# Splitting the operands of a feed-forward up projection into high and low parts in a layered attention and recurrence kernel

## What is computed

```python
for i in range(DEPTH):                      # 6 layers
    x = attn_layer(shift_tokens(x), Wqkv[i], ...) + x
    x = ffn_layer(shift_tokens(x), ...) + x
# ffn_layer:
xn = (x - mu) / sqrt(var + 1e-5) * g + bln  # 128 channels
hg = xn @ W1 + b1                           # up projection, 128 -> 2 * 341
a, gate = split(hg, 2, -1)
return a * gelu(gate) @ W2 + b2
```

## Time and profile before

| | us |
|---|---|
| median of 3 runs | 1705.56 (1705.02 to 1705.87) |
| the profiled execution: its own time | 1703.4 |
| its span, first to last instruction | 1701.6 |
| TensorE matmuls busy | 1619.4 (95%) |
| VectorE busy | 1366.9 (80%) |
| GpSimd busy | 1321.8 (78%) |
| ScalarE busy | 1308.0 (77%) |
| TensorE: all records of the up projection (L846, L847) | 171.7, in 576 records |
| mean granted TensorE clock | 0.995 |

### The profile page before, as it was taken

One profiled execution on the slowest core, in us unless ns is written; L12 is line 12 of the kernel. 1 busy time (PEld: TensorE's weight loads), 2 busy tenths in 40 slices (PEclk: granted clock), 3 DMA queues, 4 the chain that ended last, 5 costly groups with the idle time before them and its releaser, 6 DMA issues. The chain is left out here.

```text
span 1701.6 us, 49333 instructions
## 1 busy us (share of the span) xinstructions
PE 1619.4 (95%) x19632; PEld 1360.7 (80%) x19632; DVE 1366.9 (80%) x1999; ACT 1308.0 (77%) x2410; POOL 1321.8 (78%) x1269
## 2 busy tenths in 40 slices
PE   4799999999999999999999999999999999999985
PEld 2678887888888888887888887888888877787774
DVE  5888887888887888887888887888888887877843
ACT  3577788778778878878877877887887878877774
POOL 8888888887879788789788788878878777776630
PEclk9999999999999999999999999999999999999998
DMA  6233332433322333232343232334323222322231
GB/s 195 74 101 87 90 91 65 122 86 105 99 70 86 90 111 114 73 94 77 88 123 97 81 103 65 88 104 122 89 74 93 64 76 76 89 63 64 62 88 28
DMA packets 178175, 151.60 MB, mean 89 GB/s; under 512 B 110751, under 2 KB 149277, under 8 KB 177821
## 3 DMA queue, kind: packets, MB, share of 16 engines
q1 hardware_dynamic: 177948, 148.46, 30.8%
HBM read 22.06 MB, written 1.05 MB: 14 GB/s over the span
## 5 line engine op out<-in xcount | busy, mean ns | idle before, releaser
L1429 POOL TENSOR_TENSOR qk<-qk,t 128x1024 f32<-128x1024 f32 x192 | 458.8, 2390 | 108.3 <-DVE qk L1209 107.4
L1206 DVE TENSOR_TENSOR t<-ps_qn,tab 128x512 f32<-128x512 f32 x384 | 265.0, 690 | 148.9 <-ACT sq L984 136.6
L1441 POOL TENSOR_TENSOR qkr<-qk,rinv 128x1024 f32<-128x1024 f32 x192 | 361.7, 1905 | 7.5
L1020 ACT ACTIVATE qbd<-ps_tr 64x512 f32<-64x512 f32 x384 | 226.9, 591 | 72.5 <-PE ps_tr L735 67.2
L709 PE MATMUL ps_qn<-w_hi,xs_hi 128*128 128x512 f32 x576 | 261.0, 453 | 21.6 <-POOL xs_lo L1478 11.0
L971 ACT ACTIVATE pbd<-ps_tr 64x512 f32<-64x512 f32 x384 | 226.1, 589 | 66.5 <-PE ps_tr L722 63.6
L984 ACT ACTIVATE sq<-ps_qn 128x512 f32<-128x512 f32 x384 | 228.5, 595 | 43.8 <-PE ps_qn L711 38.9
L1209 DVE TENSOR_TENSOR qk<-ps_qn,tab 128x512 f32<-128x512 f32 x384 | 261.5, 681 | 0.0
L711 PE MATMUL ps_qn<-w_hi,xs_lo 128*128 128x512 f32 x576 | 228.3, 396 | 0.0
L710 PE MATMUL ps_qn<-w_lo,xs_hi 128*128 128x512 f32 x576 | 228.3, 396 | 0.0
L1219 DVE TENSOR_REDUCE ss<-sq 128x32 f32<-128x2048 f32 x96 | 216.7, 2257 | 0.0
(11 more groups left out here) (147 smaller groups left out, 3010.5 us busy)
## 6 DMA issues: line engine op xcount, KB each, us to landing
v_own<-v_new SPq DMA_DIRECT2D x96, 512.0 KB, 3.2
v_back<-v_new SPq DMA_DIRECT2D x96, 384.0 KB, 3.5
v_back<-v_own SPq DMA_DIRECT2D x96, 128.0 KB, 2.3
kT<-kT SPq DMA_DIRECT2D x84, 128.0 KB, 2.7
w_raw<-in_Wqkv SPq DMA_DIRECT2D x18, 512.0 KB, 5.3
xsh<-x SPq DMA_DIRECT2D x192, 32.0 KB, 2.3
fx<-xmid SPq DMA_DIRECT2D x96, 64.0 KB, 2.1
wo<-in_Wo SPq DMA_DIRECT2D x6, 512.0 KB, 3.8
```

Source lines behind the costliest of these rows:

```text
L1206: v.tensor_tensor(t2[:, part].rearrange("p (h s d) -> p h s d", s=2, d=DH // 2), swapped, tab[:, 2 * k + 1:2 * k + 2, :].rearrange("p o (s ...
L1429: g.tensor_tensor(qk[b][:, part], qk[b][:, part], t2[:, part], ALU.add).then_inc(added[b], 1)
L1441: g.tensor_tensor(qkr[b][:, part].rearrange("p (h d) -> p h d", d=DH), qk[b][:, part].rearrange("p (h d) -> p h d", d=DH), rinv[b][:, k * ...
```

## The change

The up projection works from split operands as the projection to q, k and v does. Per chunk half it issues three fp32r matmuls of 256 columns in place of one float32 matmul, 18 per step in place of 6.

For its input, ScalarE writes `fxn` plus bias twice in the half of stream 0, behind `round_x`: once rounded into `fxn_hi`, once in place. GpSimd no longer adds the bias. It subtracts `fxn_hi` from `fxn` into `fxn_lo` and raises `fxn_ready`, now in the half of stream 1, between `scale` and the first `add`. For the weights, ScalarE rounds all of W1 (128x682) once per layer in the half (4, 0), behind `round_fxn`, and VectorE forms the low part at the end of its half (4, 0). SyncE's wait ahead of the load of W1 is for the low part of the layer before, no longer for the fill of the bank by up chunk 2. Its wait ahead of `load_gb` keeps its text.

```diff
@@ SyncE, load_weights
-                        wait_fill(sp, qn_full, qn_order, i, ("up", 2))
+                        sp.wait_ge(w.w1_ready, l)
                         w.load_w1(sp, l)
@@ TensorE, ffn_up
-                        pe.wait_ge(w1_in, (m.layer + 1) * 32)
+                        pe.wait_ge(w.w1_ready, m.layer + 1)
                         pe.wait_ge(fxn_ready, m.n + 1)
-                    r, w = FF_CHUNKS[c]
+                    r, n = FF_CHUNKS[c]
                     bank = next_bank(i, ("up", c))
-                    mm(ps_qn[bank][0:w, 0:B * P], w1[:, r:r + w], flat(fxn), start=True, stop=True)
-                    mm(ps_qn[bank][0:w, B * P:2 * B * P], w1[:, FF + r:FF + r + w], flat(fxn),
-                       start=True, stop=True).then_inc(qn_full[bank], 1)
+                    for half_cols, first in ((slice(0, B * P), r), (slice(B * P, 2 * B * P), FF + r)):
+                        out, rows = ps_qn[bank][0:n, half_cols], slice(first, first + n)
+                        mm(out, w1_hi[:, rows], flat(fxn_hi), start=True, stop=False)
+                        mm(out, w1_hi[:, rows], flat(fxn_lo), start=False, stop=False)
+                        last = mm(out, w1_lo[:, rows], flat(fxn_hi), start=False, stop=True)
+                    last.then_inc(qn_full[bank], 1)
@@ ScalarE
+                def round_fxn(i):
+                    m = i - 4
+                    if not valid(m):
+                        return
+                    wait_fill(act, pv_done, pv_order, i - 1, ("out", 1))
+                    act.wait_ge(gb_in, (m.layer + 1) * 16)
+                    for out in (fxn_hi, fxn):
+                        f(out[:, :, :], fxn[:, :, :], ACT.Identity, bias=ln_gb[:, SM_B:SM_B + 1], scale=1.0).then_inc(fxn_high, 1)
+                def round_w1(l):
+                    act.wait_ge(w1_in, (l + 1) * 32)
+                    f(w1_hi[:, :], w1[:, :], ACT.Copy).then_inc(w.w1_high, 1)
...
                     if not rates:
                         round_x(*next_tile(i, b))
+                    if b == 0:
+                        round_fxn(i)
+                        if i.t == 4:
+                            round_w1(i.layer)
@@ VectorE
+                def low_w1(l):
+                    dve.wait_ge(w.w1_high, l + 1)
+                    v.tensor_tensor(w1_lo[:, :], w1[:, :], w1_hi[:, :].bitcast(F32), ALU.subtract).then_inc(w.w1_ready, 1)
...
                         evac_v(i, b, 5)
+                        if i.t == 4:
+                            low_w1(i.layer)
@@ GpSimd
-                def shift_fxn(i):
+                def low_fxn(i):
                     m = i - 4
                     if not valid(m):
                         return
-                    wait_fill(pool, pv_done, pv_order, i - 1, ("out", 1))
-                    pool.wait_ge(gb_in, (m.layer + 1) * 16)
-                    g.tensor_tensor(fxn[:, :, :], fxn[:, :, :], ln_gb[:, SM_B:SM_B + 1].unsqueeze(2).broadcast_to([P, B, P]),
-                                    ALU.add).then_inc(fxn_ready, 1)
+                    pool.wait_ge(fxn_high, 2 * (m.n + 1))
+                    g.tensor_tensor(fxn_lo[:, :, :], fxn[:, :, :], fxn_hi[:, :, :].bitcast(F32), ALU.subtract).then_inc(fxn_ready, 1)
@@ GpSimd, half
+                    if b == 1:
+                        low_fxn(i)
                     add(i, b, 0)
-                    if b == 0:
-                        shift_fxn(i)
-                    else:
+                    if b == 1:
                         spread_roots(i)
```

More of the change, by code:

```diff
@@ L373, in layer_tiles @@
     w.w1 = sb("w1", [P, 2 * FF])
+    w.w1_hi, w.w1_lo = (sb(f"w1_{n}", [P, 2 * FF], F32R) for n in ("hi", "lo"))
+    w.w1_high, w.w1_ready = sem("w1_high"), sem("w1_ready")
     w.w2 = sb("w2", [P, len(FF_CHUNKS), DIM])
@@ L480, in per_stream @@
             return [sb(f"{name}{b}", shape) for b in range(B)]
-        w_hi, w_lo, wo, w1, w2, ln_gb, b2, b1, rot, scales, centre_w, mean_col, ones, v_own, v_back, qbd, kT, pbd = (
-            w.w_hi, w.w_lo, w.wo, w.w1, w.w2, w.ln_gb, w.b2, w.b1, w.rot, w.scales, w.centre_w, w.mean_col, w.ones,
+        w_hi, w_lo, wo, w1, w1_hi, w1_lo, w2, ln_gb, b2, b1, rot, scales, centre_w, mean_col, ones, v_own, v_back, qbd, kT, pbd = (
+            w.w_hi, w.w_lo, w.wo, w.w1, w.w1_hi, w.w1_lo, w.w2, w.ln_gb, w.b2, w.b1, w.rot, w.scales, w.centre_w, w.mean_col, w.ones,
             w.v_own, w.v_back, w.qbd, w.kT, w.pbd)
@@ L501, in layers @@
         fc, fsq, fxn, diag = (sb(n, [P, B, P]) for n in ("fc", "fsq", "fxn", "diag"))
+        fxn_hi, fxn_lo = (sb(n, [P, B, P], F32R) for n in ("fxn_hi", "fxn_lo"))
         hid = sb("hid", [P, len(FF_CHUNKS), B, P])
@@ L546, in layers @@
             "max_ready", "exp_ready", "sum_ready", "rec_ready", "probs_ready"))
-        diag_ready, fxn_ready, gel_ready = map(sem, ("diag_ready", "fxn_ready", "gelu_ready"))
+        diag_ready, fxn_high, fxn_ready, gel_ready = map(sem, ("diag_ready", "fxn_high", "fxn_ready", "gelu_ready"))
         branch_in, rec_w, rec_wg = sem("xn_copied"), sem("rec_w_loaded"), sem("rec_gate_w_loaded")
```

## The result

The changed kernel takes 1694.6 us (median of 4 runs, 1693.3 to 1697.6), the kernel before beside it 1705.3 (4 runs): a ratio of 0.994, 95% interval 0.992 to 0.996. The forecast was 1695.5. The size is right, but the way there isn't, as the intervals show: three terms of the sum were too small by 3.5 to 4.2 us each, one of them a saving and two of them costs.

What follows compares the result with a forecast made beforehand. Ordinary steps were taken as bound by TensorE's matmuls, layer turns by GpSimd, the drain by a chain through all engines. Terms -9.9 - 2.9 - 1.6 + 0.4 + 2.4 + 1.5 = -10.1 us gave 1693.3, as a median 1695.5; range 1684 to 1704.

Steps and rivals of the forecast that it cites:

- The matmul: TensorE's up projection: each 256-column fp32r matmul takes 0.126 us, three 0.378 against 0.43, saving 0.32 us per step.
- the 0.019 left over at 512 columns: TensorE: time of a 512-column fp32r matmul (0.232 us) beyond its columns alone (0.213); taken to come once per matmul.
- The 0.116: Other reading for a 256-column matmul, if the 0.019 goes with the columns: a step saves 0.50 us, sum -16.
- That an ordinary step passes it on whole: The 31 ordinary steps among 4 to 39 shorten by TensorE's whole saving, 31 x 0.32 = 9.9 us.
- Rival A: 256-column fp32r matmuls stream at 0.111 us like the float32 pairs: 0.59 saved per step, 1685.7 us; chance 0.19.
- The turns: Five turns of a layer: TensorE's saving lost to GpSimd's chain, which sheds the 0.57 us bias operation; -2.9 us.
- The recurrence: Eight steps with the recurrence, where banks of chunks 4 and 5 wait for the up chunks' gelu: -1.6 us.
- The two thirds: Share of the step's saving counted in the eight recurrence steps: 8 x 0.2 = 1.6 us.
- The covers: Existing waits hide ScalarE's roundings, GpSimd's subtraction and W1's split at no cost, except 0.4 us once in the last layer.
- Rival B: Covers don't hold: queue costs 6, W1 5, drain 2.5 against 14.4 saved; 1704.7 us, no change; chance 0.14.
- SyncE's queue: Wait ahead of `load_gb` is met 12 us later, delaying keys and v: 0.6 us in layers 1 to 4, +2.4; ends 0 and 1.5 each.
- The drain: Steps 48 to 51: roundings ahead of q's evacuation, subtraction and up chunks ahead of `diag`; net +1.5 us, ends 0 and 2.5.

Runs made afterwards that it cites:

- f32_up: The changed kernel with the up projection in plain float32 again, added roundings, subtractions and W1 split kept, SyncE's W1 wait as before: 1711.3 us.
- w1_split_once: The changed kernel with W1 split only in layer 0, layers 1 to 5 multiplying with layer 0's parts: 1694.7 us.
- gb_wait: The changed kernel with SyncE's wait ahead of `load_gb` set to ScalarE's roundings, not the subtraction: 1688.7 us, ratio 0.990 to the kernel before.
- gb_drain: gb_wait with GpSimd's subtraction moved to the end of the half of stream 0 in the drain alone, steps 48 to 51: 1686.8 us (one run).
- gb_best: gb_drain with the last layer's W1 subtraction on GpSimd in place of VectorE: 1687.6 us, ratio 0.989 to the kernel before.

## Why the prediction was right, and where it wasn't

**The matmul (0.126; measured 0.118).** The mechanism was right, no load bound and no second pass, and the term was mis-sized. The prediction had to choose whether the 0.019 left over at 512 columns comes per matmul or with the columns, and took the first by the float32 records' example. The runs show the second: 0.112 (load-bound), 0.118 and 0.232 at 128, 256 and 512 columns. A step saved 0.43 in place of 0.32, 3.8 us over the ordinary ones. (Steps 4 to 39 have 32 of these and not 31, and the recurrence has 7 intervals and not 8, since the one into step 40 is a turn; that nearly cancels.) The 0.116 that I had named as the other reading was nearly it.

**That an ordinary step passes it on whole.** It did, but only just. Rival A (0.111, 0.59 per step) couldn't have come about at any price of the matmul: the chain through ScalarE's gelu and VectorE's gate ends the step at 31.71. That the saving stopped no sooner is luck. The prediction judged VectorE by the 0.58 that its copy of v waits for TensorE and ScalarE by the 1.66 ahead of the evacuation of q, and missed the gate ahead of that copy, whose bank TensorE needs.

**The turns (-2.9; -4.4).** The bias leaving GpSimd's chain is 0.6 per turn (f32_up), as forecast. The other 0.3 (34.77 with float32 matmuls, 34.43 with the new ones) is the matmuls' saving, most of which reaches the turn after all. The prediction had written it off there.

**The recurrence (-1.6; -3.0, and +0.8 for W1 in place of 0.4).** The two thirds were too careful: the steps passed on 0.44. The split of W1 cost what VectorE's operation takes, since nothing there hides it (w1_split_once).

**The covers.** ScalarE's two roundings, GpSimd's subtraction and the split of W1 in layers 0 to 4 cost nothing, as forecast, and ScalarE had 0.8 us more to give. Rival B fell with that in its W1 part.

**SyncE's queue (+2.4; +6.6).** The mechanism, the stretch and the two late engines were forecast, and gb_wait confirms them, but the term was mis-sized by the factor 2.8. For layer 3, the only one that was read, the times were nearly right: ScalarE was 0.76 late where the forecast had 0.6, by the forecast the last move of v lands 32.43 behind the broadcast of step 26, and VectorE's copy, which starts 0.09 behind the landing, started at 32.67. Three things made 1.4 out of the 0.6 counted. VectorE's demand was put at the time of the slow step; with the shorter one it wants the data 0.43 earlier (f32_up, with the old step, loses 0.6 to 0.9 per layer, close to the forecast). VectorE's and ScalarE's waits for TensorE were taken to absorb 0.2 of the 0.8, though TensorE behind them has nothing to absorb with. And the landing was 0.15 later. In layers 1 and 2 the copy started 0.6 later still, and no row of the kernel before could show that. The upper end, 1.5 each, holds for two of four layers.

**The drain (+1.5; +5.0).** The order of events was as forecast. In step 48, 0.33 us are lost where the clock stays up (30.47 or 30.48 in gb_wait and five others) and 1.6 where it doesn't (31.77). The last interval lost 3.7 where the forecast had 1.3. `floored` comes 1.0 later behind the broadcast than before (the matmul L838 alone takes 1.22 here and 0.70 at the full clock), the subtraction adds 0.6, and the 12 matmuls between it and the broadcast the rest: at half clock they take 2.70, where the forecast had 1.5 in place of 0.6. The kernel before had the same waits of TensorE up to that matmul (1.2 and 1.7 us), and no such stretch of the clock in its profile.

So the savings were 6.7 us larger than forecast and the costs 8.1 (queue 4.2, drain 3.5, W1 0.4), and start and end of the profiled execution add 2.8. That puts the execution 4.3 us above its forecast of 1693.3. But the median is 3.0 below this execution, where I had put it 2.2 above mine: 4.3 - 3.0 - 2.2 = -0.9, which is the miss of the median. The forecast's closeness is in part luck.

## What to carry to other kernels

When a producer's signal moves to another place, look for every waiter on it, also those in queues whose text isn't touched: here one such wait took back about 6 of 16 us, and pointing it at the operation that it really needed returned them. When the bound engine gets faster, follow each bank it waits for back through the engine that frees it, and ask how long that engine, and the one that it waits for, have run without a gap; the idle time that it shows further on isn't cover. A chain placed well in the steady part may be badly placed in the drain, where the order of GpSimd's last operations decides.

## What the runs showed of the hardware

- fp32r matmuls in a stream, from start to start: 0.232 us at 512 columns, 0.118 at 256, 0.112 at 128 with 128 rows of output and 0.076 with 85. The last two go with the size of the weights.
- TensorE's clock: in the drain, up to the last broadcast, stretches at 1.2 GHz in the profiles of the changed kernel and its variants, none in that of before. The windows of gb_wait, gb_drain and gb_best (same columns as above) for the last interval, and for step 48 of gb_best:

```profile
1647.10:1661.20 14.10, 7.12 (x34) 0.78 0.04 9
```
```profile
1646.40:1658.10 11.70, 7.41 (x35) 0.81 0.05 11
```
```profile
1593.10:1624.90 31.80, 26.86 (x385) 0.95 0.39 113
...
1648.30:1660.40 12.10, 7.79 (x33) 0.75 0.05 11
```

  They come where TensorE waits often, and not in each execution at the same place: gb_drain and gb_best, with the same work in the drain, take 64.1 and 67.3 us for it. What decides it is open.
- The spare VectorE operation of 128x256 took 1.45 to 1.75 us in steps 4 to 47 and 0.36, 0.64, 0.41 and 0.67 in the drain. In all of steps 4 to 47 GpSimd's `qk` addition was running when it started, and it ended 0.3 behind the end of that addition. In steps 49 and 51 another GpSimd operation was running, and it ended 0.3 behind that one. In steps 48 and 50 none was, and it took the 0.35 to 0.40 that was expected. So its length is that of the GpSimd operation it meets and not of its own size. That is read from these 48 times; no run was made to separate it, and VectorE's subtraction of 128x682 took 0.86 beside short GpSimd operations. VectorE, then GpSimd, in step 21, and VectorE in step 48:

```profile
724.23 1.48 DVE L1402 TENSOR_TENSOR spare<-ident 128x256 f32<-128x256 f32 x1
```
```profile
723.04 2.38 POOL L1461 TENSOR_TENSOR qk<-qk,t 128x1024 f32<-128x1024 f32 x1 [0.72 <-DVE qk L1233]
```
```profile
1664.98 0.36 DVE L1402 TENSOR_TENSOR spare<-ident 128x256 f32<-128x256 f32 x1
```
